# A block-masked linear layer and a LoRA mixture on eight cores: an explicit activation table load, Ln and Exp for Sqrt, and the mask multiply on another engine

## The chip, the cores and the metric

The kernel runs on all 8 cores of one Trainium2 chip. Each core does the same program on its own 2048 of the 16384 tokens; the weights are read whole by every core. The metric is the device time of the slowest core, in microseconds (us).

## The reference

Two layers, each with a residual and a layernorm behind it. The first is a linear layer whose weight is kept only in those 32 x 32 blocks in which the mask is on. The second is a dense linear layer plus a mixture of rank-16 adapters with a top-2 router over 8 experts.

```python
bm = mask.reshape(Nb, BH, Kb, BW).sum(axis=(1, 3)) > 0
w  = (weight.reshape(Nb, BH, Kb, BW) * bm[:, None, :, None]).reshape(N, K)
x = _layernorm(x + einsum('bsk,nk->bsn', x, w) + bias)       # N = K = 4096
# layer 2, on the layernormed x
probs = softmax(x @ Wr.T); top-2, renormalised -> w          # 8 experts
lora = einsum('ter,te,eor->to', einsum('ti,eri->ter', x, A), w, Bm) * 2.0
x = _layernorm(x + x @ Wb.T + bias + lora)
# _layernorm(x) = (x - mean) / sqrt(var + 1e-5)
```

## The kernel before

A core takes its 2048 tokens in three chunks of 768, 768 and 512, that is 6, 6 and 4 token tiles of 128. A chunk goes through these stages: load and transpose the input (`input_chunk`), layer 0 (`layer_pass(0, ...)`), the first layernorm with a transposition and the router for each tile, layer 1 (`layer_pass(1, ...)`), the second layernorm with the output.

A layer pass runs over 16 groups of 256 output columns (`nci`). For each group and token tile it does a bias matmul (L447), 32 matmuls over the contraction (L452), in layer 1 one more for the adapters (L461), and then on VectorE an add of the residual (L472) and statistics (L476). The weights of a group stand in one of two buffers `wtb`. Chunk 0 makes them; it also writes them to DRAM (`wts`), from where chunks 1 and 2 read them ready made.

Making the weights of a group, in chunk 0, means two tiles of 128 weight rows (`gen_subtile`, `ntt`), each in one of two buffers `wstg`:

- GpSimd issues the load of the tile (L377, which casts to bf16) once the transposes of the tile two before are done.
- In layer 0, GpSimd then waits for that load and for `q2full`, and multiplies the tile by the block mask (L385). The mask value of a block is broadcast over its 32 columns.
- TensorE transposes the tile in four steps of eight transposes (`gen_transposes`, L406) into one of two PSUM buffers `pT`, and ScalarE copies each step into `wtb` (L419). So a group has eight such steps. The next but one step waits for the copy.

`maskpipe` makes `q2full` for a tile: VectorE sums the mask over 32 columns (L328), a matmul sums over 32 rows (L340), VectorE compares with 0 (L347), a matmul spreads it over the rows again (L354), VectorE copies it out (L361). Four tiles are done ahead of the first group; after the matmuls of group n the tiles 2n+4 and 2n+5 follow.

`ln_stats_apply` is the layernorm of a token tile: VectorE makes mean and variance (L609) and adds epsilon (L612), ScalarE takes the square root (L619), VectorE the reciprocal (L626) and minus mean times it (L628), ScalarE applies both to the tile (L667, or in four quarters with an output transfer for each, L650). The router uses an Exp on ScalarE (L706).

[...] Nearly every `@block.scalar` call holds a single ACTIVATE. The program before names no activation table; the loads in the trace were put in by the compiler. Engines wait for counters (`sT` TensorE, `sV` VectorE, `sC` ScalarE, `sP` GpSimd).

Of the kernel before, what the change touches and what calls it, by code (L numbers as in the profile page):

```python
# [14 lines left out]
AF = mybir.ActivationFunctionType  # L15
# [24 lines left out]
def build_program(t_core, chunk_sizes):  # L40
# [3 lines left out]
    nc = bass.Bass("TRN2", target_bir_lowering=False)  # L44
# [29 lines left out]
    with contextlib.ExitStack() as st:  # L74
# [8 lines left out]
        sV = sem("sV")  # L83
        sC = sem("sC")
        sP = sem("sP")
# [14 lines left out]
        def gdma(g, dst, src):  # L100
            return _qdma(sGs, gidx, g, dst, src)
# [4 lines left out]
        def sdma(q, dst, src):  # L106
            return _qdma(sSs, gidx2, q, dst, src)
# [33 lines left out]
        stdt = [sbuf("stdt0", [128, 1], F32), sbuf("stdt1", [128, 1], F32)]  # L141
        rstd = [sbuf("rstd0", [128, 1], F32), sbuf("rstd1", [128, 1], F32)]
# [18 lines left out]
        pH = psum("pH", [128, 512], F32)  # L161

        block = st.enter_context(nc.Block())

        state = {
            "pt_free": [None, None],
# [142 lines left out]
        q2_ready = [0] * KT  # L309
# [57 lines left out]
        def gen_subtile(L, ntt):  # L367
            sl = ntt % 2
            wsrc = w0 if L == 0 else wb
            fw = state["wstg_free"][sl]  # L370
            gres = [None]

            @block.gpsimd
            def _(g, ntt=ntt, sl=sl, wsrc=wsrc, fw=fw):
                if fw is not None:
                    g.wait_ge(fw[0].h, fw[1])
                gres[0] = gdma(g, wstg[sl][:, :],  # L377
                               wsrc[ntt * 128:(ntt + 1) * 128, :])
            gs, gv = gres[0]
            if L == 0:  # L380
                @block.gpsimd
                def _(g, ntt=ntt, sl=sl, gs=gs, gv=gv, q2v=q2_ready[ntt]):
                    g.wait_ge(gs.h, gv)
                    g.wait_ge(sV.h, q2v)
                    sP.inc(g.tensor_tensor(  # L385
                        wstg[sl][:, :].rearrange("p (kb j) -> p kb j", j=32),
                        wstg[sl][:, :].rearrange("p (kb j) -> p kb j", j=32),
                        q2full[:, ntt * 128:(ntt + 1) * 128]
                        .unsqueeze(2).broadcast_to([128, 128, 32]),
                        ALU.mult))  # L390
                return (sP, sP.n)
            return (gs, gv)

        def gen_transposes(nci, sub, ready):
# [87 lines left out]
        def layer_pass(L, c, nt, lora, lora_gate=None):  # L482
# [3 lines left out]
            for nci in range(NNC):  # L486
                sl = nci % 2
                if c == 0:
                    subs = []
                    for sub in range(2):  # L490
                        ntt = nci * 2 + sub
                        ready = gen_subtile(L, ntt)
                        ev = gen_transposes(nci, sub, ready)
                        subs.append(ev)
# [105 lines left out]
        def ln_stats_apply(i, iset, evac_wait, write_out=None, t0=0):  # L600
            lf = state["ln_free"][iset]

            @block.vector
            def _(v, i=i, iset=iset, evac_wait=evac_wait, lf=lf):
                if evac_wait:
                    v.wait_ge(sV.h, evac_wait)
                if lf is not None:
                    v.wait_ge(lf[0].h, lf[1])
                sV.inc(v.bn_aggr(mv[iset][:, :],  # L609
                                 bnbt[:, i * 96:(i + 1) * 96]))  # L610
                v.wait_ge(sV.h, sV.n)
                sV.inc(v.tensor_scalar(vpe[iset][:, :], mv[iset][:, 1:2],  # L612
                                       EPS, None, ALU.add))
            ve_v = sV.n

            @block.scalar
            def _(sc, iset=iset, ve_v=ve_v):
                sc.wait_ge(sV.h, ve_v)
                sC.inc(sc.activation(stdt[iset][:, :], vpe[iset][:, :],  # L619
                                     AF.Sqrt))  # L620
            sq_v = sC.n

            @block.vector
            def _(v, iset=iset, sq_v=sq_v):
                v.wait_ge(sC.h, sq_v)
                sV.inc(v.reciprocal(rstd[iset][:, :], stdt[iset][:, :]))  # L626
                v.wait_ge(sV.h, sV.n)
                sV.inc(v.tensor_scalar(nmb[iset][:, :], mv[iset][:, 0:1],  # L628
                                       rstd[iset][:, 0:1], -1.0,
                                       ALU.mult, ALU.mult))  # L630
            ab_v = sV.n

            applies = []
            if write_out is not None:
                ofree = state.setdefault("outstg_free", [None, None, None])
                for qt in range(4):
                    slo = state.setdefault("outslot", [0])
                    k = slo[0] % 3
                    slo[0] += 1
                    ob = outstg[k]  # L640
                    of = ofree[k]

                    @block.scalar
                    def _(sc, i=i, iset=iset, ab_v=ab_v, qt=qt, ob=ob,
                          of=of):
                        if qt == 0:
                            sc.wait_ge(sV.h, ab_v)
                        if of is not None:
                            sc.wait_ge(of[0].h, of[1])
                        sC.inc(sc.activation(  # L650
                            ob[:, :],
                            xnat[:, i * D + qt * 1024:i * D + (qt + 1) * 1024],
                            AF.Identity, bias=nmb[iset][:, 0:1],
                            scale=rstd[iset][:, 0:1]))
                        sc.wait_ge(sC.h, sC.n)
                        sdma(sc,
                             write_out[t0 + i * 128:t0 + (i + 1) * 128,
                                       qt * 1024:(qt + 1) * 1024],
                             ob[:, :])
                    ofree[k] = (sSs[(gidx2[0] - 1) % NS],  # L660
                                sSs[(gidx2[0] - 1) % NS].n)
                    applies.append(sC.n)
            else:
                @block.scalar
                def _(sc, i=i, iset=iset, ab_v=ab_v):
                    sc.wait_ge(sV.h, ab_v)
                    sC.inc(sc.activation(  # L667
                        xnat[:, i * D:(i + 1) * D],
                        xnat[:, i * D:(i + 1) * D],
                        AF.Identity, bias=nmb[iset][:, 0:1],  # L670
                        scale=rstd[iset][:, 0:1]))
                applies.append(sC.n)
            state["ln_free"][iset] = (sC, sC.n)
            return applies
# [207 lines left out]
```

## Time and profile before

| | us |
|---|---|
| three runs | 3625.4, 3696.1, 3754.28 (median 3696.1) |
| the profiled execution | 3620.43 |
| its span, slowest core (7) | 3618.9 |
| spans of the 8 cores | 3595.7 to 3618.9 |

The profile is of one execution on the slowest core. A time in a timeline or a chain is counted from the start of the span. A busy time is the sum of an engine's instructions. The granted clock is TensorE's, as a share of its full speed. The stages on this core: layer 0 of chunk 0 from about 166 to 1052 us, the first layernorm to about 1160, layer 1 of chunk 0 to about 1898, the output to about 2002, and chunks 1 and 2 in the rest, of 3618.9 us.

### The profile page before, as it was taken

The page shows a single profiled execution, that of the slowest core. Times are in us where ns is not written, and L with a number is a line of the kernel's source. Part 1 is how long each engine was busy: PE and PEld are TensorE (multiplying, and loading weights), DVE is VectorE, ACT ScalarE, POOL GpSimd, SP SyncE. Part 2 cuts the span into 40 slices and gives each one's busy share as a digit, 9 for nine tenths or more (in the row PEclk, how much of TensorE's full clock was granted, in tenths as well). Part 3 has the DMA queues.
Part 4 walks back from the last instruction along what each step waited for, and adds up shares of the span by engine and source line. Part 5 has one row for each costly group of instructions (what it writes and reads, how often), then busy time and mean ns, then how long its engine had stood idle before and what let it go on. Part 6 is the DMA issues. An engine that isn't in the chain of part 4 may idle for free.

```text
span 3618.9 us, 49582 instructions; the slowest of 8 cores (3595.7 to 3618.9 us)
## 1 busy us (share of the span) xinstructions
PE 2466.3 (68%) x21109; PEld 1981.1 (55%) x21109; DVE 759.7 (21%) x1573; ACT 904.8 (25%) x768; POOL 316.6 (9%) x190
## 2 busy tenths in 40 slices
PE   2356565655653777777761999946999739967991
PEld 1245353444442555555551788835888628846881
DVE  1332222313122111111111222232222212222220
ACT  0223324242333444444437000031000150021005
POOL 2233232222200000000000000000000000000000
PEclk6677676767776777777775999967999869978996
DMA  9565556565420444444448233310333455532452
GB/s 110 113 107 117 105 107 112 107 125 100 99 48 1 95 95 95 95 95 95 95 100 219 76 94 92 95 41 25 96 86 86 124 160 142 143 97 61 133 144 93
DMA packets 264260, 364.03 MB, mean 101 GB/s; under 512 B 38626, under 2 KB 173794, under 8 KB 249570
## 3 DMA queue, kind: packets, MB, share of 16 engines
q0 software_dynamic: 50224, 119.63, 20.9%
q1 hardware_dynamic: 204602, 207.66, 20.4%
q10 hardware_dynamic: 9216, 33.56, 2.4%
q8 instruction: 170, 2.79, 0.3%
q14 instruction: 48, 0.39, 0.0%
HBM read 377.69 MB, written 102.76 MB: 133 GB/s over the span
## 4 chain that ended last, share of the span: by engine, by line
PE 61%; ACT 22%; DVE 6%; DMA 5%; issue 4%; ACTq 1%; POOL 1%; DVEq 0%; SPq 0%; POOLq 0%
PE pmm L452 53%; ACT L419 8%; ACT wtb L419 7%; DVE bs2t L328 4%; PE pmm L447 3%; PE pT L566 2%; ACT xnat L667 2%; DMA out<-outstg 2%; ACT L650 2%; ACT outstg L650 2%; DMA xnat<-xin 1%; ACT L619 1%; PE pH L807 1%; DMA mstg<-mask 1%; PE pmm L461 1%
## 5 line engine op out<-in xcount | busy, mean ns | idle before, releaser
L452 PE MATMUL pmm<-wtb,x1t 128*128 128x256 bf16 x16384 | 1934.5, 278 | 0.0
L452 PEld LDWEIGHTS pmm<-wtb,x1t 128*128 128x128 bf16 x16384 | 1590.5, 100 | 266.6 <-issue 7.5
L472 DVE SCALAR_TENSOR_TENSOR xnat<-pmm,xnat 128x256 bf16<-128x256 f32 x512 | 217.5, 425 | 2215.8 <-PE pmm L452 1108.1
L419 ACT ACT_TABLE_LOAD x256 | 328.4, 1283 | 1143.7 <-PE pT L406 1139.7
L406 PE MATMUL pT<-ident,wstg 128*128 128x128 bf16 x2048 | 230.4, 287 | 299.0 <-ACT wtb L419 281.9
L619 ACT ACT_TABLE_LOAD x32 | 41.1, 1283 | 1395.4 <-DVE vpe L612 1387.9
L406 PEld LDWEIGHTS pT<-ident,wstg 128*128 128x128 bf16 x2048 | 182.2, 129 | 343.1 <-issue 340.9
L566 PE MATMUL pT<-ident,xnat 128*128 128x128 bf16 x1024 | 106.4, 282 | 325.6 <-ACT xnat L667 142.9
L566 PEld LDWEIGHTS pT<-ident,xnat 128*128 128x128 bf16 x1024 | 89.7, 128 | 342.2 <-issue 339.3
L419 ACT ACTIVATE wtb<-pT 128x1024 bf16<-128x1024 bf16 x256 | 262.2, 1024 | 2.8
L385 POOL TENSOR_TENSOR wstg<-wstg,q2full 128x4096 bf16<-128x4096 bf16 x32 | 225.4, 7044 | 335.3 <-DMA wstg<-w 293.6
L447 PE MATMUL pmm<-wtb,ones 1*128 1x256 bf16 x512 | 145.1, 283 | 126.1 <-ACT wtb L419 124.0
L476 DVE BATCH_NORM_STATS2 bnbt<-xnat 128x6 f32<-128x256 bf16 x512 | 218.7, 427 | 52.8
L447 PEld LDWEIGHTS pmm<-wtb,ones 1*128 1x128 bf16 x512 | 46.6, 91 | 234.9 <-issue 234.9
L328 DVE TENSOR_REDUCE bs2t<-mstg 128x128 f32<-128x4096 bf16 x32 | 141.0, 4407 | 3.4 <-DMA mstg<-mask 3.3
L340 PE MATMUL pQ<-bs2t,e4tf 128*4 128x128 f32 x64 | 18.7, 395 | 172.9 <-DVE bs2t L328 172.9
L577 DVE COPY x1t<-pT 128x1024 bf16<-128x1024 bf16 x128 | 86.8, 690 | 143.6 <-PE pT L566 143.4
L94 POOL DMA_DIRECT2D xnat<-xin x16 | 8.5, 536 | 1135.7 <-ACT outstg L650 1109.1
L340 PEld LDWEIGHTS pQ<-bs2t,e4tf 128*4 128x4 f32 x64 | 3.7, 83 | 179.3 <-issue 179.3
L650 ACT ACT_TABLE_LOAD x64 | 82.1, 1283 | 44.1 <-ACT outstg L650 21.5
L94 POOL DMA_DIRECT2D wstg<-wb x32 | 17.3, 540 | 794.9 <-PE pT L406 794.9
L650 ACT ACTIVATE outstg<-xnat,nmb,rstd 128x1024 f32<-128x1024 bf16 x64 | 79.3, 1239 | 0.8
(58 smaller groups left out, 489.3 us busy)
## 6 DMA issues: line engine op xcount, KB each, us to landing
wts<-wtb SPq DMA_DIRECT2D x32, 2112.0 KB, 13.1
mstg<-mask POOLq DMA_DIRECT2D x32, 1024.0 KB, 9.5
wstg<-w POOLq DMA_DIRECT2D x32, 1024.0 KB, 10.9
wstg<-wb POOLq DMA_DIRECT2D x32, 1024.0 KB, 8.9
out<-outstg ACTq DMA_DIRECT2D x64, 512.0 KB, 3.3
xnat<-xin POOLq DMA_DIRECT2D x16, 1024.0 KB, 10.9
wstg<-am POOLq DMA_DIRECT2D x1, 1024.0 KB, 10.8
wstg<-bm POOLq DMA_DIRECT2D x8, 128.0 KB, 10.4
```

What stands on the lines that cost most here:

```text
L328: sV.inc(v.tensor_reduce(bs2t[sl][:, :].unsqueeze(2), mstg[sl][:, :].rearrange("p (kb j) -> p kb j", j=32), AX, ALU.add))
L385: sP.inc(g.tensor_tensor(wstg[sl][:, :].rearrange("p (kb j) -> p kb j", j=32), wstg[sl][:, :].rearrange("p (kb j) -> p kb j", j=32), q2ful ...
L406: mm = t.transpose(pT[k][:, j * 128:(j + 1) * 128], wstg[sl2][:, kt * 128:(kt + 1) * 128], ident[:, :])
L419: sC.inc(sc.activation(wtb[slw][:, :].rearrange("p (kt n) -> p kt n", n=NCW) [:, gp * 8:(gp + 1) * 8, sub * 128:sub * 128 + 128], pT[kk][: ...
L447: t.matmul(pmm[bk][:, 0:NCW], ones1[0:1, :], wtb[sl][0:1, KT * NCW:KT * NCW + NCW], start=True, stop=False)
L452: mm = t.matmul(pmm[bk][:, 0:NCW], x1t[:, kt * maxchunk + i * 128: kt * maxchunk + (i + 1) * 128], wtb[sl][:, kt * NCW:(kt + 1) * NCW], st ...
L472: sV.inc(v.scalar_tensor_tensor(sl_ap, pmm[bk][:, 0:NCW], 1.0, sl_ap, ALU.mult, ALU.add))
L476: sV.inc(v.bn_stats(bnbt[:, i * 96 + nci * 6:i * 96 + (nci + 1) * 6], sl_ap))
L566: mm = t.transpose(pT[k][:, j * 128:(j + 1) * 128], xnat[:, i * D + kt * 128:i * D + (kt + 1) * 128], ident[:, :])
L577: sV.inc(v.tensor_copy(x1t[:, :].rearrange("p (kt t) -> p kt t", t=maxchunk) [:, gp * 8:(gp + 1) * 8, i * 128:(i + 1) * 128], pT[kk][:, :] ...
L619: sC.inc(sc.activation(stdt[iset][:, :], vpe[iset][:, :], AF.Sqrt))
L650: sC.inc(sc.activation(ob[:, :], xnat[:, i * D + qt * 1024:i * D + (qt + 1) * 1024], AF.Identity, bias=nmb[iset][:, 0:1], scale=rstd[iset] ...
```

## The change

Three edits. At the start of the program a block for ScalarE holds one explicit load of the table set `natural_log_exp_and_others`. The layernorm takes 1/sqrt(v) as Exp(-0.5 Ln(v)): two ACTIVATEs on ScalarE, with a wait between them, instead of a Sqrt there and a reciprocal on VectorE. The mask multiply of layer 0 is issued on VectorE instead of GpSimd, at the same place in the code, with the same waits, and counts on VectorE's counter.

```diff
         block = st.enter_context(nc.Block())
 
+        @block.scalar
+        def _(sc):
+            from concourse.hw_specs import get_activation_tables
+            for idx, (nm, funcs) in enumerate(
+                    get_activation_tables(nc.m.arch).items()):
+                if nm == "natural_log_exp_and_others":
+                    sc.add_instruction(mybir.InstLoadActFuncSet(
+                        name=nc.get_next_instruction_name(),
+                        act_func_set_id=idx, ins=[], outs=[]))
+                    break
+
@@ gen_subtile
             if L == 0:
-                @block.gpsimd
-                def _(g, ntt=ntt, sl=sl, gs=gs, gv=gv, q2v=q2_ready[ntt]):
-                    g.wait_ge(gs.h, gv)
-                    g.wait_ge(sV.h, q2v)
-                    sP.inc(g.tensor_tensor(
+                @block.vector
+                def _(v, ntt=ntt, sl=sl, gs=gs, gv=gv, q2v=q2_ready[ntt]):
+                    v.wait_ge(gs.h, gv)
+                    v.wait_ge(sV.h, q2v)
+                    sV.inc(v.tensor_tensor(
                         wstg[sl][:, :].rearrange("p (kb j) -> p kb j", j=32),
                         wstg[sl][:, :].rearrange("p (kb j) -> p kb j", j=32),
                         q2full[:, ntt * 128:(ntt + 1) * 128]
                         .unsqueeze(2).broadcast_to([128, 128, 32]),
                         ALU.mult))
-                return (sP, sP.n)
+                return (sV, sV.n)
             return (gs, gv)
@@ ln_stats_apply
             def _(sc, iset=iset, ve_v=ve_v):
                 sc.wait_ge(sV.h, ve_v)
                 sC.inc(sc.activation(stdt[iset][:, :], vpe[iset][:, :],
-                                     AF.Sqrt))
+                                     AF.Ln))
+                sc.wait_ge(sC.h, sC.n)
+                sC.inc(sc.activation(rstd[iset][:, :], stdt[iset][:, :],
+                                     AF.Exp, scale=-0.5))
             sq_v = sC.n
@@
                 v.wait_ge(sC.h, sq_v)
-                sV.inc(v.reciprocal(rstd[iset][:, :], stdt[iset][:, :]))
-                v.wait_ge(sV.h, sV.n)
                 sV.inc(v.tensor_scalar(nmb[iset][:, :], mv[iset][:, 0:1],
```

## Rows read from the trace of the kernel before

**Rows 1.** The page, busy time and share of the span of each engine.

```profile
PE 2466.3 (68%) x21109; PEld 1981.1 (55%) x21109; DVE 759.7 (21%) x1573; ACT 904.8 (25%) x768; POOL 316.6 (9%) x190
```

**Rows 2.** Windows by stage: stretch, length, busy and count per engine, granted clock, DMA share, GB/s.

```profile
166.00:1052.00 886.00, 532.30 (x4212) 412.60 (x4212) 220.01 (x280) 278.75 (x243) 250.07 (x103) 0.72 0.55 109
...
1160.00:1898.00 738.00, 524.41 (x4351) 416.21 (x4349) 83.08 (x195) 295.32 (x256) 23.68 (x45) 0.79 0.43 93
...
2002.00:2376.00 374.00, 367.54 (x3168) 302.27 (x3167) 82.90 (x196) 3.61 (x4) 0.00 (x0) 0.99 0.32 92
```

**Rows 3.** Groups by line on ScalarE: busy, mean ns; idle before, and its releaser.

```profile
L419 ACT ACT_TABLE_LOAD x256 | 328.4, 1283 | 1143.7 <-PE pT L406 1139.7
L419 ACT ACTIVATE wtb<-pT 128x1024 bf16<-128x1024 bf16 x256 | 262.2, 1024 | 2.8
L650 ACT ACT_TABLE_LOAD x64 | 82.1, 1283 | 44.1 <-ACT outstg L650 21.5 <-DVE nmb L628 12.0 <-DMA out<-outstg 10.6
...
L619 ACT ACT_TABLE_LOAD x32 | 41.1, 1283 | 1395.4 <-DVE vpe L612 1387.9 <-ACT outstg L650 7.5
L667 ACT ACT_TABLE_LOAD x16 | 20.5, 1283 | 10.6 <-DVE nmb L628 10.6
L706 ACT ACT_TABLE_LOAD x16 | 20.5, 1283 | 103.1 <-DVE tlr L699 103.1
```

**Rows 4.** Timeline, one column group of layer 0, chunk 0: start, length, idle before.

```profile
645.73 7.04 POOL L385 TENSOR_TENSOR wstg<-wstg,q2full 128x4096 bf16<-128x4096 bf16 x1 [11.45 <-DMA wstg<-w]
...
662.29 4.41 DVE L328 TENSOR_REDUCE bs2t<-mstg 128x128 f32<-128x4096 bf16 x1
...
668.07 0.26 PE L354 MATMUL pQ<-bm4t,e4b 4*128 4x128 bf16 x1 [0.53 <-DVE bm4t L347]
...
668.31 1.86 PE L406 MATMUL pT<-ident,wstg 128*128 128x128 bf16 x16
...
671.80 1.28 ACT L419 ACT_TABLE_LOAD   x1
...
671.92 1.01 PE L406 MATMUL pT<-ident,wstg 128*128 128x128 bf16 x8 [1.75 <-ACT wtb L419]
...
688.49 0.37 PE L447 MATMUL pmm<-wtb,ones 1*128 1x256 bf16 x1 [3.87 <-ACT wtb L419]
```

**Rows 5.** Timeline of the start, up to the first matmul of layer 0.

```profile
131.55 0.29 DVE L361 CAST q2full<-pQ 128x128 bf16<-128x128 f32 x1 [0.51 <-PE pQ L354]
137.30 0.59 POOL L94 DMA_DIRECT2D wstg<-w  x1
...
148.13 7.04 POOL L385 TENSOR_TENSOR wstg<-wstg,q2full 128x4096 bf16<-128x4096 bf16 x1 [10.24 <-DMA wstg<-w]
...
166.09 0.36 PE L447 MATMUL pmm<-wtb,ones 1*128 1x256 bf16 x1 [3.77 <-ACT wtb L419]
```

**Rows 6.** The page's groups on VectorE and GpSimd whose operands are nearest.

```profile
L385 POOL TENSOR_TENSOR wstg<-wstg,q2full 128x4096 bf16<-128x4096 bf16 x32 | 225.4, 7044 | 335.3 <-DMA wstg<-w 293.6
...
L328 DVE TENSOR_REDUCE bs2t<-mstg 128x128 f32<-128x4096 bf16 x32 | 141.0, 4407 | 3.4 <-DMA mstg<-mask 3.3
...
L577 DVE COPY x1t<-pT 128x1024 bf16<-128x1024 bf16 x128 | 86.8, 690 | 143.6 <-PE pT L566 143.4
```

**Rows 7.** Chain of waits, whole span: two cold first matmul groups of layer 1.

```profile
1689.48 6.48 PE pmm L452 x32
...
1870.39 6.48 PE pmm L452 x32
```

**Rows 8.** Chain of waits, first layernorm of chunk 0, one tile.

```profile
1049.43 1.28 ACT L619
...
1051.59 1.28 ACT L667
```

**Rows 9.** Timeline of the output stage of chunk 0: two tiles.

```profile
1928.23 1.28 ACT L619 ACT_TABLE_LOAD   x1 [0.56 <-ACT outstg L650]
...
1943.05 1.28 ACT L619 ACT_TABLE_LOAD   x1 [0.56 <-ACT outstg L650]
```

## The prediction

> **What bounds the kernel now.** I read the page's busy times first. TensorE is busy 68% of the span, VectorE 21%, ScalarE 25%, GpSimd 9% [rows 1]. No engine is full, so the question is where TensorE stands still. The windows by stage answer it: chunk 1's layer 0 is at TensorE's limit (367.5 of 374 us busy, granted clock 0.99), but chunk 0 is not. Its layer 0 has TensorE busy for 532 of 886 us at 0.72, its layer 1 for 524 of 738 us at 0.79 [rows 2]. These are the stages in which the weights are made: 16 column groups each, 32 in all.
>
> A group of layer 0 takes (688.49 - 166.09) / 9 = 58.0 us, from the first matmul of group 0 [rows 5] to that of group 9 [rows 4]. A group of layer 1 takes (1870.39 - 1689.48) / 4 = 45.2 us [rows 7]. In both, the transposes and their copies out take from 668.31 to 688.49 us, 20.2 us for eight steps [rows 4]. The eight steps do not go at TensorE's pace: eight transposes take 1.01 us and then wait 1.75 us for ScalarE. ScalarE's step is a table load of 1.28 us and a copy of 1.02 us, 2.34 us with the gaps between them. The load stands on that path, between the end of one copy and the start of the next. The ScalarE groups show a load for every one of the 384 ACTIVATEs: 256 + 64 + 32 + 16 + 16 [rows 3].
>
> In layer 0 there is a second hole: VectorE reduces two mask tiles (L328, 4.41 us each) after its last work on a group, and the transposes start at 668.31, right behind the small matmul of the second one (668.07 + 0.26) [rows 4]. The mask multiply is not in any hole. GpSimd starts the odd tile's at 645.73 and ends at 652.77, and its transposes come only behind four others, later than 668 [rows 4].
>
> **The change, part by part.**
>
> *The explicit table load.* If it did away with the other loads it would be worth a great deal (first rival). I take it that it does away with none. The rows show a load before every ACTIVATE, even between two copies of the same function at the same line [rows 3, 4]: whoever places them carries nothing over from one `@block.scalar` to the next. Each of these holds one ACTIVATE. The new load stands in a block of its own with no ACTIVATE in it, so a placer that starts anew in each block sees none of it. Cost: one load of 1.28 us at the start, where ScalarE waits until 138 us for its first work anyway. Worth 0.
>
> [...]
>
> *Ln and Exp for Sqrt and the reciprocal, 32 times.* In the block of L619 there are now two ACTIVATEs behind the block's load. The Exp (bound by the Sqrt's 0.20 us) and a wait of about 0.1 us take the place of a reciprocal of 0.16 us on VectorE and its wait. That is 0 to 0.1 us each, at most 3 us; I take 0. It needs one load for both functions; were it two, it would be 32 x 1.28 = 41 us (second rival).
>
> *The mask multiply, 32 times, from GpSimd to VectorE.* The trace has no such instruction on VectorE. The bounds: from below a VectorE copy of bf16, 1024 elements in 0.69 us [rows 6], four of them 2.8 us; from above GpSimd's own 7.04 us [rows 6]. [...] I take 4.42 us.
>
> [...]
>
> Where it lies matters more than its length. VectorE works in order. The multiplies of the next group are now issued behind this group's evacuations and both mask reduces. So the even tile's starts when the last cast (L361, behind the matmul that ends at 668.33) is done, about 668.8, and ends at 673.3; the transposes now start then and not at 668.31. That is 5.1 us per group, on the path, with nothing beside it on TensorE. The odd tile's multiply (4.5 us more) is hidden: four steps of 2.34 us go ahead of its transposes. Behind the multiplies in VectorE's queue stand only the evacuations of the next group, over 15 us later. Groups 1 to 15 pay: 15 x 5.1 = +76.5 us (group 15 has no reduces ahead of it, but waits for its multiply all the same).
>
> GpSimd's queue gets free: it no longer waits for a weight tile before it issues the next one's load, nor the bias and mask loads behind it. In steady state these had slack already (645.73 against 668), so 0. At the start it counts. There the second weight load was issued at 137.30, behind the first multiply, and the second multiply began at 148.13 [rows 5]. Now that load goes out at once and lands by about 141 at the latest. VectorE multiplies the first tile from 131.9 (its last cast ends at 131.84 [rows 5]) to 136.4 and the second by 145.5. Transposes start at 136.5, eight steps of 2.34 us and 1.8 us around them give the first matmul at 157 where it was 166.09: -9 us.
>
> **Sum.** 3620.4 us for the profiled execution (its span is 3618.9) + 76.5 - 9 = **3688 us**, +1.9%. That execution lies at the low end of the runs shown (3625 to 3754, median 3696); the forecast is on its scale. I call 2% the least that a measurement of this kernel can tell from no change.
>
> **The rivals.**
>
> *Faster: one load of the program's own switches the placing off for the whole program.* Then all 384 loads go; Ln, Exp and Identity would have to be in one set, and the rewrite makes that possible. For it: that the rows cannot tell a placer of blocks from one that steps aside once it finds a load. Against it: the memoryless pattern of [rows 3, 4]. Price: a step falls from 2.34 to about 1.15 us, half of a buffer's cycle (1.01 transposes, 1.02 copy, two handovers of some 0.13), so eight steps save 9.6 us; 32 groups give -307. The multiply still costs +76.5, since the odd tile's (4.5 us) just fits beside four steps (4.6 us); the start gains 6 more (-15 in all). In the first layernorm two loads per tile stand on the chain [rows 8] and a little of a third: 16 x 2.8 = -45. In the output stage a tile takes 1943.05 - 1928.23 = 14.8 us [rows 9] with five loads, 6.4 us; output transfers would then set the pace, so I take 4 us of it: 16 x 4 = -64. Sum: 3620.4 - 307 + 76.5 - 15 - 45 - 64 = **3266 us**. The unknown is TensorE's clock: the first 32 matmuls of a group take 6.48 us in the cold groups shown [rows 7]; were transposes dense enough to raise the clock early, up to 1.5 us more per group would come back. It spans 3220 to 3330.
>
> *Slower: the block of Ln and Exp gets two loads.* +41 us, 3729 us. It decides at once, as the chain waits for ScalarE in every layernorm. Against it: the second function would have to be outside of the set loaded for the first.
>
> *Slower: VectorE multiplies at GpSimd's pace.* 7.04 us for 4.42: 15 x 2.6 = +39, 3727 us. With the fast end, 2.8 us, it is 15 x 1.6 = -24, 3664 us. Both are ends of the forecast's own range.
>
> **How the numbers follow.** Loads stay, one per block: 0.52. Loads gone: 0.39. Loads stay and 32 more come: 0.05. The rest, 0.04, is contention that I cannot place, between them. The likeliest case gives 3688, with its own range 3655 to 3730. Since the second case holds far more than 2 in 10, the range must reach it: 3225 to 3730. The likeliest case straddles the 2% line at 3693; with the middle price it stays just below. Of its 0.52 I give 0.30 to within 2% and 0.22 to slower. Faster: 0.39 + 0.01. Within: 0.30 + 0.02. Slower: 0.22 + 0.05 + 0.01.
>
> **What would show it.** Right: ScalarE still shows 256 loads at the wtb copies and steps of 2.34 us; a column group of layer 0 takes 63.1 us and one of layer 1 still 45.2; the multiply on VectorE lasts 4.4 us and is what the first transposes wait for; the first matmul starts near 157 us; GpSimd loses 225 us of busy time. Wrong: a count of one load in all, with layer 1's groups at about 35.6 us, ends the forecast in favour of the first rival. [...]

## The result and the profile after

| | before | changed |
|---|---|---|
| median of ten runs, us | 3626.4 | 3264.5 |
| profiled execution's span, us | 3618.9 | 3258.5 |

Some executions of each kernel take some per cent longer, with a lower granted clock on the cores of one die; they are in the medians, and the ratios and their intervals leave them out. The ratio is 0.9003, 95% interval 0.8991 to 0.9014: ten per cent faster. The profiled execution of the changed kernel took 3260.1 us, and the forecast for it was 3688. The first rival, "one load of the program's own switches the placing off for the whole program", had been worked out to 3266.

The page of the changed kernel, span and busy times ([rows 1] before):

```profile
span 3258.5 us, 49199 instructions; the slowest of 8 cores (3238.7 to 3258.5 us)
...
PE 2412.2 (74%) x21109; PEld 1945.9 (60%) x21109; DVE 893.3 (27%) x1573; ACT 405.5 (12%) x417; POOL 90.7 (3%) x158
```

ScalarE's busy time went from 904.8 to 405.5 us, GpSimd's from 316.6 to 90.7, VectorE's from 759.7 to 893.3. ScalarE's groups by line, where [rows 3] stood before (busy us, mean ns, idle before and its releaser):

```profile
L430 ACT ACTIVATE wtb<-pT 128x1024 bf16<-128x1024 bf16 x256 | 247.8, 1021 | 1216.9 <-PE pT L417 1215.8 <-issue 0.9
L662 ACT ACTIVATE outstg<-xnat,nmb,rstd 128x1024 f32<-128x1024 bf16 x64 | 79.3, 1239 | 94.4 <-DMA out<-outstg 65.4 <-ACT outstg L662 21.3 <-DVE nmb L640 7.7
L679 ACT ACTIVATE xnat<-xnat,nmb,rstd 128x4096 bf16<-128x4096 bf16 x16 | 60.8, 3799 | 6.6 <-DVE nmb L640 6.6
L633 ACT ACTIVATE rstd<-stdt 128x1 f32<-128x1 f32 x32 | 6.5, 203 | 2.9
L630 ACT ACTIVATE stdt<-vpe 128x1 f32<-128x1 f32 x32 | 6.5, 203 | 1414.5 <-DVE vpe L623 1406.9 <-ACT outstg L662 7.7
L718 ACT ACTIVATE exr<-tlr 128x8 f32<-128x8 f32 x16 | 3.3, 209 | 103.7 <-DVE tlr L711 103.7
L171 ACT ACT_TABLE_LOAD x1 | 1.3, 1283 | 1.1 <-PEq L44 1.1
```

L171 is the explicit load, now the only one; the 384 of before are gone. The copies into `wtb` (L430, L419 before) have none before them, nor has any other ACTIVATE. The new Exp (L633) costs 203 ns, 32 times.

A column group of layer 0, chunk 0, in the timeline ([rows 4] before):

```profile
557.82 0.26 PE L365 MATMUL pQ<-bm4t,e4b 4*128 4x128 bf16 x1 [0.54 <-DVE bm4t L358]
...
558.40 8.75 DVE L396 TENSOR_TENSOR wstg<-wstg,q2full 128x4096 bf16<-128x4096 bf16 x2
...
563.07 1.86 PE L417 MATMUL pT<-ident,wstg 128*128 128x128 bf16 x16 [4.98 <-DVE wstg L396]
564.23 1.94 ACT L430 ACTIVATE wtb<-pT 128x1024 bf16<-128x1024 bf16 x2 [44.80 <-PE pT L417]
...
565.39 1.93 PE L417 MATMUL pT<-ident,wstg 128*128 128x128 bf16 x16 [0.47 <-ACT wtb L430]
...
568.89 3.87 ACT L430 ACTIVATE wtb<-pT 128x1024 bf16<-128x1024 bf16 x4 [0.39 <-PE pT L417]
...
573.11 0.37 PE L458 MATMUL pmm<-wtb,ones 1*128 1x256 bf16 x1 [1.53 <-ACT wtb L430]
```

The transposes no longer start behind the mask's last matmul (557.82) but 5.0 us after it has ended, at 563.07: they wait for the first of the two multiplies on VectorE. From there, two copies run back to back and a pair of steps takes 565.39 - 563.07 = 2.32 us where one step took 2.34. The last four steps go faster still, four copies in 3.87 us. The matmuls start 573.11 - 563.07 = 10.0 us after the first transpose; before it was 20.2. From 149.45 us, the first matmul of group 0 in the same view, to 573.11, that of group 8, a group takes 53.0 us; before 58.0.

The same in layer 1, timeline and, below it, the chain of waits over the whole span (start, length), four groups apart:

```profile
1269.36 1.06 PE L417 MATMUL pT<-ident,wstg 128*128 128x128 bf16 x16
...
1270.12 7.72 ACT L430 ACTIVATE wtb<-pT 128x1024 bf16<-128x1024 bf16 x8 [26.19 <-PE pT L417]
...
1272.20 0.61 PE L417 MATMUL pT<-ident,wstg 128*128 128x128 bf16 x8 [0.31 <-ACT wtb L430]
...
1278.19 0.26 PE L458 MATMUL pmm<-wtb,ones 1*128 1x256 bf16 x1 [1.53 <-ACT wtb L430]
```

```profile
1210.68 5.22 PE pmm L463 x32
...
1346.28 5.27 PE pmm L463 x32
```

Eight copies of 1.02 us, overlapping a little, take 7.72 us: 0.965 us a step, ScalarE's own pace. A group takes (1346.28 - 1210.68) / 4 = 33.9 us, before 45.2 [rows 7].

Where the 360 us went, by the start of the first matmul in each stage on the profiled core:

| stretch | before, us | changed, us | difference |
|---|---|---|---|
| start to first matmul of layer 0 | 166.1 | 149.5 | -16.6 |
| to first matmul of layer 1 (layer 0, first layernorm) | 1026.2 | 928.9 | -97.3 |
| to first matmul of chunk 1 (layer 1, output, input) | 809.4 | 628.3 | -181.2 |
| to the end (chunks 1 and 2) | 1617.2 | 1551.9 | -65.3 |

### The profile page after: what moved, and what is told of

Its sections match the earlier page's. It is cut to its first block, busy times and chain, and to the rows that moved or that the text cites. A ratio compares the mean times of both kernels' runs of the same rounds, so it can differ in the third digit from the quotient of the medians.

```text
span 3258.5 us, 49199 instructions; the slowest of 8 cores (3238.7 to 3258.5 us)
## 1 busy us (share of the span) xinstructions
PE 2412.2 (74%) x21109; PEld 1945.9 (60%) x21109; DVE 893.3 (27%) x1573; ACT 405.5 (12%) x417; POOL 90.7 (3%) x158
## 4 chain that ended last, share of the span: by engine, by line
PE 69%; DVE 9%; ACT 9%; DMA 6%; issue 4%; ACTq 1%; POOL 0%; DVEq 0%; SPq 0%; POOLq 0%
PE pmm L463 58%; ACT wtb L430 6%; DVE bs2t L339 4%; PE pmm L458 3%; DMA out<-outstg 3%; DVE wstg L396 2%; PE pT L577 2%; PE pT L417 2%; ACT xnat L679 2%; ACT outstg L662 1%; DMA xnat<-xin 1%; PE pH L819 1%; DMA mstg<-mask 1%; PE pmm L472 1%; DMA wstg<-w 1%
## 5 line engine op out<-in xcount | busy, mean ns | idle before, releaser
L430 ACT ACTIVATE wtb<-pT 128x1024 bf16<-128x1024 bf16 x256 | 247.8, 1021 | 1216.9 <-PE pT L417 1215.8
L417 PE MATMUL pT<-ident,wstg 128*128 128x128 bf16 x2048 | 188.5, 254 | 149.1 <-DVE wstg L396 83.0
L417 PEld LDWEIGHTS pT<-ident,wstg 128*128 128x128 bf16 x2048 | 153.3, 114 | 183.6 <-issue 177.9
L630 ACT ACTIVATE stdt<-vpe 128x1 f32<-128x1 f32 x32 | 6.5, 203 | 1414.5 <-DVE vpe L623 1406.9
L339 DVE TENSOR_REDUCE bs2t<-mstg 128x128 f32<-128x4096 bf16 x32 | 141.0, 4408 | 4.7 <-DMA mstg<-mask 4.4
L396 DVE TENSOR_TENSOR wstg<-wstg,q2full 128x4096 bf16<-128x4096 bf16 x32 | 140.1, 4418 | 2.4 <-DMA wstg<-w 2.4
L662 ACT ACTIVATE outstg<-xnat,nmb,rstd 128x1024 f32<-128x1024 bf16 x64 | 79.3, 1239 | 94.4 <-DMA out<-outstg 65.4
L472 PE MATMUL pmm<-bmft,g_t 128*128 128x256 bf16 x256 | 69.8, 273 | 0.0
L679 ACT ACTIVATE xnat<-xnat,nmb,rstd 128x4096 bf16<-128x4096 bf16 x16 | 60.8, 3799 | 6.6 <-DVE nmb L640 6.6
L640 DVE TENSOR_SCALAR nmb<-mv,rstd 128x1 f32<-128x1 f32 x32 | 6.8, 214 | 160.0 <-ACT rstd L633 160.0
```

The costliest lines, as they stand in the source:

```text
L339: sV.inc(v.tensor_reduce(bs2t[sl][:, :].unsqueeze(2), mstg[sl][:, :].rearrange("p (kb j) -> p kb j", j=32), AX, ALU.add))
L396: sV.inc(v.tensor_tensor(wstg[sl][:, :].rearrange("p (kb j) -> p kb j", j=32), wstg[sl][:, :].rearrange("p (kb j) -> p kb j", j=32), q2ful ...
L417: mm = t.transpose(pT[k][:, j * 128:(j + 1) * 128], wstg[sl2][:, kt * 128:(kt + 1) * 128], ident[:, :])
L430: sC.inc(sc.activation(wtb[slw][:, :].rearrange("p (kt n) -> p kt n", n=NCW) [:, gp * 8:(gp + 1) * 8, sub * 128:sub * 128 + 128], pT[kk][: ...
L472: mm = t.matmul(pmm[bk][:, 0:NCW], lora[:, i * 128:(i + 1) * 128], bmft[:, nci * NCW:(nci + 1) * NCW], start=False, stop=True)
L662: sC.inc(sc.activation(ob[:, :], xnat[:, i * D + qt * 1024:i * D + (qt + 1) * 1024], AF.Identity, bias=nmb[iset][:, 0:1], scale=rstd[iset] ...
```

## The experiments

Theory A: a load of the program's own anywhere turns off the compiler's placing for all of the program. Rival B: the loads went because after the rewrite one table set serves every function. The rest of the runs price the parts. Next to them the kernel before came out at 3628.5 to 3629.5 us, so times of different runs are compared below to within a few us.

### Ln and Exp alone

```diff
-                                     AF.Sqrt))
+                                     AF.Ln))
+                sc.wait_ge(sC.h, sC.n)
+                sC.inc(sc.activation(rstd[iset][:, :], stdt[iset][:, :],
+                                     AF.Exp, scale=-0.5))
...
-                sV.inc(v.reciprocal(rstd[iset][:, :], stdt[iset][:, :]))
-                v.wait_ge(sV.h, sV.n)
```

> The kernel before with only the Ln and Exp in place of Sqrt and the reciprocal; no explicit load, multiply on GpSimd. Theory A (the program's own load is what turns the compiler's placing off): 384 loads stay, one for Ln and Exp together, steps of the weight copies stay at 2.34 us; within 3 us of before, ratio 1.00. Theory B (the loads went because after the rewrite one table set serves every function, so the placer needs only one): one load or a few, ScalarE steps near 1 us, some 330 to 430 us less, ratio 0.88 to 0.91. If Ln and Exp got a load each: 416 loads and +41 us, ratio 1.011.

Measured: 3628.2 us, ratio 0.9989 (0.995 to 1.0028). ScalarE's groups by line:

```profile
L619 ACT ACT_TABLE_LOAD x32 | 41.1, 1283 | 1396.1 <-DVE vpe L612 1388.9 <-ACT outstg L651 7.2
...
L419 ACT ACT_TABLE_LOAD x256 | 328.4, 1283 | 1146.6 <-PE pT L406 1142.7
```

All 256 loads at the copies stay, and the block of Ln and Exp has one load, 32 in all. Rival B falls: the rewrite takes no load away. It also costs nothing that this run can measure, as the prediction's second part had it. None of the 384 loads of this trace (256 + 64 + 32 + 16 + 16) stands in the kernel's source, so all were placed by the compiler, and it placed one for both functions of that block: Ln and Exp, 203 ns each, come behind it.

### The explicit load alone

The kernel before with the block of the explicit load alone (shortened here):

```diff
+        @block.scalar
+        def _(sc):
+            ... InstLoadActFuncSet of natural_log_exp_and_others ...
```

> The kernel before with only the explicit load at the start; Sqrt and the reciprocal stay. The loaded set holds no Sqrt, so the layernorm's factor is not the reference's; everything else is computed. Theory A1 (any load of the program's own turns the placing off, without a look at which functions follow): one load in the trace, multiply on GpSimd, the time of the kernel with load, Ln, Exp and that multiply, 3200 us, ratio 0.88. Theory A3 (the placer still puts a load where the set in force lacks the function): 33 or more loads at the square roots, 3200 + 40.

Measured: 3194.1 us, ratio 0.8799 (0.8781 to 0.8816). ScalarE's groups:

```profile
L630 ACT ACTIVATE stdt<-vpe 128x1 f32<-128x1 f32 x32 | 6.5, 203 | 1416.7 <-DVE vpe L623 1409.3 <-ACT outstg L661 7.4
...
L171 ACT ACT_TABLE_LOAD x1 | 1.3, 1283 | 1.1 <-PEq L44 1.1
```

One load, and none at the 32 square roots. The set in force does not serve them: the relative error of this kernel's output is 1.0, and with Ln and Exp in place of Sqrt and the reciprocal, and otherwise the same, the kernel computes the reference's result. So no load came even where one was needed (A1, not A3). The Sqrt runs in the same 203 ns as before. With Ln and Exp the time is 3199.9 us (the run with the multiply back on GpSimd, below; single executions 3195.0 to 3214.7), so they bring no time: with them the one load of that run's trace serves every function used.

### The explicit load late

The kernel is the changed one, but its single load stands in the first layernorm's block, behind the 128 copies of layer 0:

```diff
                 sc.wait_ge(sV.h, ve_v)
+                if late[0]:
+                    load_set(sc)
+                    late[0] = False
                 sC.inc(sc.activation(stdt[iset][:, :], vpe[iset][:, :],
```

> The changed kernel with its single explicit load not at the start but in the ScalarE block of the first layernorm, behind the 128 weight copies of layer 0 (which run with no table loaded by this program, so the result need not be the reference's). Theory A1 (any load of the program's own anywhere turns the placing off for the whole program): one load in the trace, at about 980 us, none ahead of it, groups of layer 0 at 53 us, the time of the changed kernel, ratio 0.90. Theory A2 (it is off only from that load on): 129 loads, groups of layer 0 at 63 us, layer 1 at 34 us, about 3264 + 150, ratio 0.94.

Measured: 3264.7 us for the profiled execution, the one to compare (another took 3362.8), where the changed kernel's took 3260.1 and its median is 3264.5. ScalarE's groups, then its timeline around the load:

```profile
L431 ACT ACTIVATE wtb<-pT 128x1024 bf16<-128x1024 bf16 x256 | 248.0, 1021 | 1224.5 <-PE pT L418 1223.3 <-issue 0.7
...
L170 ACT ACT_TABLE_LOAD x1 | 1.3, 1283 | 27.0 <-DVE vpe L624 27.0
```

```profile
935.65 1.94 ACT L431 ACTIVATE wtb<-pT 128x1024 bf16<-128x1024 bf16 x2 [0.40 <-PE pT L418]
964.62 1.28 ACT L170 ACT_TABLE_LOAD   x1 [27.03 <-DVE vpe L624]
965.91 0.20 ACT L634 ACTIVATE stdt<-vpe 128x1 f32<-128x1 f32 x1
```

The load comes at 964.62 us, and the copies ahead of it have none either. A1 holds and A2 falls: in this run it is not "from the load on" (129 loads), it is the whole program (1 load). The prediction's picture of a placer that carries nothing from block to block fits the trace of before, but it was the wrong question: in all runs with a load of their own, no load was added anywhere.

### The loads back at the weight copies

```diff
                     if scrw is not None:
                         sc.wait_ge(scrw[0].h, scrw[1])
+                    load_set(sc)
                     sC.inc(sc.activation(
                         wtb[slw] ...
```

> The changed kernel with the explicit load also in front of each of the 256 weight copies, behind their waits, as the compiler had it. Theory (the gain is the sum of the loads on the chain, most of it at these copies): steps go back to 2.34 us, groups of layer 1 from 33.9 to 45.2 us (+11.3), groups of layer 0 from 53.3 to 63.9 as in the kernel with the multiply alone (+10.6): 3264 + 16 x 11.3 + 16 x 10.6 = 3614 us, ratio 0.996. Rival (the gain came as much from elsewhere, the instruction stream or the transfers): under +250, ratio under 0.97.

Measured: 3625.5 us, ratio 0.9988 (0.9953 to 1.0022), expected 3614. The chain of waits shows layer 1's groups as before, (1581.10 - 1400.19) / 4 = 45.2 us:

```profile
1400.19 6.46 PE pmm L474 x32
...
1581.10 6.46 PE pmm L474 x32
```

So 256 loads account for 3625.5 - 3264.5 = 361 us, 1.41 us each: more than the load's 1.28. The two rows are the slowest of a cycle of four groups; between them the first 32 matmuls of a group take 5.55, 5.12 and 4.91 us in the same view.

### The loads back everywhere else

Edit: `load_set(sc)` ahead of the ACTIVATEs of L630, L679, L718 and L662 of the changed kernel, 128 loads.

> The changed kernel with the explicit load in front of each ACTIVATE of the layernorms (one for Ln and Exp together), the router and the output, 128 loads; the weight copies have none. By the first rival's terms: 16 x 2.8 in the first layernorm and 16 x 4 in the output stage, +109: 3373 us, ratio 0.930. By what is left of the difference between the multiply alone (3717) and the changed kernel (3264), 453, after 350 at the weight copies: +103. If output transfers set the pace of the output stage with or without loads: +45 alone, ratio 0.912.

Measured: 3352.4 and 3352.8 us for the two executions of four that can be compared (the other two took 3394.6 and 3438.0), too few for an interval. Against 3264.5 that is +88 us, not +109 and not +45. The sum closes: 361 and 88 us are 449, and the multiply alone, with all its loads, is 3706.9 (the middle one of three executions, below) - 3264.5 = 442 us above the changed kernel. The changed kernel's own output stage shows why it is less than 109. ScalarE's timeline in chunk 0 and, below it, in chunk 2:

```profile
1622.01 0.20 ACT L630 ACTIVATE stdt<-vpe 128x1 f32<-128x1 f32 x1 [0.79 <-ACT outstg L662]
...
1633.60 1.24 ACT L662 ACTIVATE outstg<-xnat,nmb,rstd 128x1024 f32<-128x1024 bf16 x1 [5.76 <-DMA out<-outstg]
...
1635.41 0.20 ACT L630 ACTIVATE stdt<-vpe 128x1 f32<-128x1 f32 x1 [0.57 <-ACT outstg L662]
```

```profile
3221.40 0.20 ACT L630 ACTIVATE stdt<-vpe 128x1 f32<-128x1 f32 x1 [0.57 <-ACT outstg L662]
...
3229.89 0.20 ACT L630 ACTIVATE stdt<-vpe 128x1 f32<-128x1 f32 x1 [0.57 <-ACT outstg L662]
```

In chunk 0 a tile takes 1635.41 - 1622.01 = 13.4 us (before 14.8 [rows 9]): the fourth quarter waits 5.76 us for an output transfer to free its buffer. Of five loads' 6.4 us only 1.4 come back. In chunk 2, where no input load runs beside it, a tile takes 3229.89 - 3221.40 = 8.5 us, 6.3 less than the 14.8 of [rows 9]. The DMA engines are busy 0.88 of the stretch in chunk 0 (1609 to 1690 us) and 0.47 in chunk 2 (3213 to 3258 us). In the run with the loads back, a tile of the output stage takes 15.7, 14.8 and 14.6 us in the three chunks, on average, where the changed kernel takes 13.6, 13.5 and 8.3; a tile of the first layernorm takes 18.1 to 18.2 where it takes 15.5 to 15.7. That gives 6 x 2.1 + 6 x 1.4 + 4 x 6.3 = 46 us and 16 x 2.6 = 41 us, 87 together.

### Half of the loads at the copies

Edit: as in the run with 256, but only for odd steps (`if gp % 2:`), 128 loads.

> The changed kernel with the explicit load in front of every second weight copy (128 loads). If each load costs what it adds to its step (linear): half of what 256 loads cost (3625 - 3264 = 361), that is +180, 3445 us, ratio 0.949, groups of layer 1 at 39.6 us. If TensorE's clock carries part of the gain (with full loads it stands at 0.79 in layer 1, without at 0.93, and transposes take 0.61 instead of 1.01 us per eight): the cost is not linear; where half the loads already let the clock fall, groups of layer 1 come near 41 us and the time near 3480; where the clock holds, near 38.5 and 3430.

Measured: 3478.8 us, ratio 0.9582 (0.9563 to 0.9602), +214 us where half of 361 would be 180. The chain of waits, 14 groups apart, gives (1793.88 - 1220.45) / 14 = 41.0 us a group (linear would be 39.6):

```profile
1220.45 6.09 PE pmm L475 x32
...
1793.88 6.10 PE pmm L475 x32
```

TensorE's timeline within a group shows where the rest comes from (16, 8, 8 and 16 transposes; idle before in brackets):

```profile
1368.96 1.06 PE L427 MATMUL pT<-ident,wstg 128*128 128x128 bf16 x16
1370.89 0.61 PE L427 MATMUL pT<-ident,wstg 128*128 128x128 bf16 x8 [0.87 <-ACT wtb L442]
1373.23 0.61 PE L427 MATMUL pT<-ident,wstg 128*128 128x128 bf16 x8 [1.73 <-ACT wtb L442]
...
1376.48 1.93 PE L427 MATMUL pT<-ident,wstg 128*128 128x128 bf16 x16 [1.73 <-ACT wtb L442]
...
1383.91 0.37 PE L470 MATMUL pmm<-wtb,ones 1*128 1x256 bf16 x1 [2.81 <-ACT wtb L442]
```

The first 32 transposes of this group (1368.96 to 1373.84) still take 0.61 us per eight or less, at a granted clock of 1.00; the sixteen at 1376.48 take 1.93 us, at 0.50, after two pauses of 1.73 us. And the matmuls behind them need 6.10 us for 32 in both rows of the chain where the changed kernel needs 5.27. Four loads per group cost 7.1 us (41.0 - 33.9), 1.8 us each; eight cost 11.3, 1.4 each. Of the 7.1 us, 0.8 stand in those 32 matmuls and 6.1 between the first transpose and the matmuls: 1383.91 - 1368.96 = 15.0 us here, 1278.19 - 1269.36 = 8.8 in the changed kernel. With all eight loads the 32 matmuls take 5.5 us on average. The mean granted clock of layer 1 in this run is 0.83 (1200 to 1750 us), much nearer to the 0.79 of the run with 256 loads (1300 to 1900 us) than to the changed kernel's. The windows of the two main stages before and after (stretch, then busy time of TensorE, its weight loads, VectorE, ScalarE and GpSimd; granted clock third from the end); before:

```profile
170.00:1000.00 830.00, 494.51 (x3906) 382.63 (x3904) 212.56 (x262) 258.40 (x224) 246.83 (x99) 0.71 0.56 110
1200.00:1850.00 650.00, 464.94 (x3909) 372.72 (x3907) 74.97 (x176) 258.40 (x224) 22.10 (x42) 0.80 0.44 94
```

changed:

```profile
160.00:900.00 740.00, 460.77 (x3704) 357.52 (x3702) 328.38 (x276) 108.69 (x112) 35.76 (x68) 0.76 0.57 118
1100.00:1600.00 500.00, 437.64 (x3978) 353.70 (x3976) 75.64 (x178) 115.87 (x120) 22.05 (x42) 0.96 0.59 129
```

Layer 1's granted clock rises from 0.80 to 0.96, layer 0's from 0.71 to 0.76 only, for there TensorE still waits 4.97 us for the second reduce and 4.98 us for the multiply, and the sixteen transposes at 563.07 run at a clock of 0.50, 1.86 us. In the last run below, where both waits are gone, it is 0.91 in layer 0 (160 to 700 us).

### The multiply alone on VectorE

Edit: only the change's last part, on the kernel before.

> The kernel before with only the multiply on VectorE. Both theories on the loads: 384 stay. By the prediction's sum: multiply 4.42 us, +5.1 us in each of 15 groups, -9 us at the start: 3620 + 67.5, ratio 1.0186. Rival D (the multiply hides, or the earlier weight loads pay for it): ratio 1.00 to 1.005.

Measured: 3717.3 us (three executions of 3705.5 to 3727.8, one of 3761.9), ratio 1.0225 (1.0167 to 1.0283): slower, though the interval does not settle whether by more than 2%. Its profiled span is 3704.0, +85 us. The chain of waits, 14 groups apart, gives (1058.34 - 164.50) / 14 = 63.8 us a group:

```profile
164.50 6.40 PE pmm L452 x32
...
1058.34 4.96 PE pmm L452 x32
```

That is +5.8 us a group, not +5.1. The multiply itself came out as taken; the page's group in the changed kernel:

```profile
L396 DVE TENSOR_TENSOR wstg<-wstg,q2full 128x4096 bf16<-128x4096 bf16 x32 | 140.1, 4418 | 2.4 <-DMA wstg<-w 2.4
```

The rest stands in the matmuls: behind the longer pause the first 32 of a group take 4.9 to 6.5 us, 5.7 on average, in before mostly 5.0 to 5.1. The start did not bring the 9 us: the first bias matmul is at 164.14 and not at 157, since the last mask's cast ended at 139.54, 7.7 us later than before, behind later mask loads (the first is issued at 79.74 us, before at 72.50); from that cast to the matmul it is 24.6 us for 34.3, so the mechanism of the start holds. Rival D (it hides) falls.

### The multiply back on GpSimd

Edit: the changed kernel with L396 in a GpSimd block, as before.

> The changed kernel with the mask multiply put back on GpSimd. Theory A: all but one load stay away, so the whole gain of the loads shows and the multiply's price is gone: in 15 groups of layer 0 the transposes start right behind the mask's last matmul (-5.1 us each, -76), while the first group starts later again (GpSimd loads the second tile behind its first multiply, first matmul at about 160 instead of 149.5, +11): about 3264 - 65 = 3199 us, ratio to before 0.882. Rival C (GpSimd's chain of load, 7.0 us multiply, load, multiply becomes the bound once groups are shorter): a group cannot be shorter than some 41 us, it will be about 48, so it should not bind; if it does the ratio stays at 0.90 or above.

Measured: 3199.9 us, ratio 0.8806 (0.8763 to 0.885). The chain of waits, ten groups apart: (643.02 - 165.58) / 10 = 47.7 us a group, GpSimd's chain does not bind:

```profile
165.58 5.47 PE pmm L463 x32
...
643.02 5.27 PE pmm L463 x32
```

So the multiply's move costs 3264.5 - 3199.9 = 65 us of the change (the four executions lie between 3195.0 and 3214.7). Its first part brought some 427 us (362 + 65), its third gave 65 back.

### A version that beats both

The two mask reduces move between the evacuations, and GpSimd, which has the multiply again, gets both weight loads ahead of its two multiplies (shortened, with comments added):

```diff
+                        def hook(i, mq=mq, mg=mg, mr=mr):
+                            if i in (0, 2):
+                                mr[i // 2] = mp_reduce(mq[i // 2], mg[i // 2])
                     nci_matmuls(..., hook=hook)     # called behind L487
+                    for j, q in enumerate(mq):
+                        mp_rest(q, mr[j])           # the two matmuls and casts
...
-                    for sub in range(2):
-                        ready = gen_subtile(L, nci * 2 + sub)
+                    ld = [gen_subtile(L, nci * 2 + sub) for sub in range(2)]
+                    rdy = [gen_mult(L, nci * 2 + sub, ld[sub]) for sub in range(2)]
```

> A version meant to beat both: one explicit load, Ln and Exp, multiply on GpSimd with both weight loads issued ahead of the two multiplies, and the two mask reduces of a group issued on VectorE behind the evacuations of the token tiles 0 and 2 instead of behind the last, with the rest of the mask work behind the matmuls as before. If the reduces (4.4 us each) find room between evacuations (0.95 us every 3.8 us of matmuls): a group of layer 0 goes from about 47.6 to about 38 us, 14 groups, -135 from 3200: 3065 us, and the first group starts some 10 us earlier: ratio 0.843. If a late evacuation holds TensorE by 1 to 2 us per reduce: 3110. If GpSimd's two loads and two multiplies, about 4.6 + 11 + 14 us after the transposes of the first tile, do not fit: groups over 40 us, ratio over 0.86.

Measured: 3051.9 us, ratio 0.8411 (0.8394 to 0.8427), 6.5% below the changed kernel. The timeline of a group:

```profile
500.69 4.40 DVE L343 TENSOR_REDUCE bs2t<-mstg 128x128 f32<-128x4096 bf16 x1
...
508.30 4.40 DVE L343 TENSOR_REDUCE bs2t<-mstg 128x128 f32<-128x4096 bf16 x1
...
518.68 0.09 PEld L358 LDWEIGHTS pQ<-bs2t,e4tf 128*4 128x4 f32 x2 [0.21 <-issue]
...
522.04 1.81 PE L431 MATMUL pT<-ident,wstg 128*128 128x128 bf16 x16
...
531.63 0.26 PE L472 MATMUL pmm<-wtb,ones 1*128 1x256 bf16 x1 [1.53 <-ACT wtb L444]
```

The reduces run at 500.69 and 508.30, beside matmuls. The mask's matmuls start at 518.68 right behind the last token tile, the transposes at 522.04. From 494.18 to 531.63, matmul to matmul, a group takes 37.5 us. The two edits were not run apart, so what each brings is open.

## Why the prediction was wrong

**The failed step** is the first part of the change. The prediction said that the rows show "a load before every ACTIVATE", that "whoever places them carries nothing over from one `@block.scalar` to the next", and from this that "a placer that starts anew in each block sees none of it": worth 0. The rows were read rightly. The inference was not sound: how the loads are placed when the program has none says nothing about whether they are placed when it has one. The prediction named that gap under its first rival ("the rows cannot tell a placer of blocks from one that steps aside") and still gave the reading of memoryless rows the larger chance. Three runs settle it: with the load alone there is 1 load in the trace, with the load late 1, with Ln and Exp alone 384. In place of the 0 the explicit load is worth 3626.4 - 3199.9 = 427 us, taken with Ln and Exp, which bring none of it. All three traces without a load of the program's own (before, Ln and Exp alone, the multiply alone) show 384 loads; in none with one does a load stand that the program did not issue itself.

**The rival's own sum** (3266) came within 2 us of the median and 6 of the profiled execution, but not term by term, so that closeness is in part luck. The copies' steps in layer 0 fell to 1.16 us as taken (1.15) in the first half of a group and to 0.97 in the second, in layer 1 to 0.965, as the transposes there run at a granted clock of 1.00 (1269 to 1278 us), 0.61 us per eight: a group of layer 1 gained 11.3 us, not 9.6, 27 us more over 16 groups. Little came back in the matmuls behind them, where the prediction saw up to 1.5 us: [rows 7] show the slowest of a cycle of four groups, 6.48, 5.60, 5.16 and 4.93 us, 5.5 on average, and the changed kernel takes 5.27. The first layernorm gave 15.5 to 15.7 for 18.0 to 18.3 us per tile, some 2.6 and not 2.8. The output stage gave 1.3 and 1.9 us per tile in chunks 0 and 1 and 6.3 in chunk 2, about 44 in all and not 64; in the first two the transfers do set the pace, more sharply than taken. The start: 16.6 for 15. One row was misread: the 1.75 us that TensorE waits at 671.92 is only the first of its waits in the group, the steady one is 1.32 (1.01 and 1.32 make the step of 2.33); no sum used it.

**The multiply.** 4.42 us taken, 4418 ns measured. No row of before shows such a multiply on VectorE: the 4.42 us was the author's estimate, next to the reduce's 4.41 us [rows 6], and the reduce takes 4408 ns in the changed kernel. Its place in VectorE's order is as described: the next group's multiply needs no result of these two reduces, yet it starts at 558.40, behind the cast at 558.19, and 5.0 us lie between the mask's last matmul and the transposes. Alone it cost 5.8 us a group and not 5.1, for the slower first matmuls behind the longer pause (5.7 us for 5.1) were left out; in the changed kernel, taken back, 65 us.

**Ln and Exp.** Costed at 0 to 3 us; the run shows no difference that can be measured.

**The second and third rivals.** Two loads in the block of Ln and Exp: no, 32 in the run with the rewrite alone. GpSimd's pace on VectorE: no.

**The range.** It ran from 3225 to 3730 because two cases with chances of 0.52 and 0.39 lay on both sides of no change, and the time fell in it. The direction named was that of the wrong case. No run shows a multiply fast enough for the lower end of the likeliest case, 3655: that is (3688 - 3655) / 15 = 2.2 us less in a group, and the fastest of the 32 multiplies took 4407 ns.

## What to carry to other kernels

A load in front of every ACTIVATE is worth a look. Here there were 384, in a program whose ScalarE blocks nearly all hold one ACTIVATE, and each cost more than its 1.28 us at the copies, where ScalarE is the step between two others (1.41), and less where a transfer set the pace (in the output stage of chunk 0, 1.4 of five loads' 6.4 us came back). One explicit load removed them all, but then none came for a function that the set in force does not serve either (Sqrt, relative error 1.0). Work moved from an engine that is hidden to one that is on the path has to be placed in the other's order, not only added to its busy time: the multiply cost 65 us behind the reduces, while the reduces, moved between evacuations together with an earlier weight load, took a group from 47.7 to 37.5 us. When a rival of ten per cent hangs on what a tool does and not on the chip, the profile before cannot price its chance, and the text should not let a pattern in it decide.

## What the runs showed that I had not expected

The price of a short stall on ScalarE was not its length. A load of 1.283 us costs 1.41 us on the chain when all eight steps have one and 1.8 us when four have. In the run with four, TensorE's granted clock goes from 1.00 to 0.50 within the group's transposes, behind pauses of 1.73 us, and the next 32 matmuls take 6.10 us; with eight they take 5.5 on average, without loads 5.27. That the clock makes the difference is read off these traces; no run changes the clock and nothing else.
